# First layer's attention of a two-layer cross-attention kernel: scores in four 32-row strips, and another order of work round them

## What is computed

```python
def _L0_xattn_ref(q, latent_kv, Wq, Wkv_expand, Wout):   # q = layernorm(x), latent_kv = ctx_512 (first 100 rows matter: causal)
    NH, HD = 16, 16
    qp = q @ Wq.T
    kv = latent_kv @ Wkv_expand.T
    k, v = jnp.split(kv, 2, axis=-1)
    qh, kh, vh = [t.reshape(b, -1, NH, HD).transpose(0, 2, 1, 3) for t in (qp, k, v)]
    scores = jnp.einsum('bhqd,bhkd->bhqk', qh, kh) * inv_sqrt_d
    scores = jnp.where(causal, scores, jnp.finfo(scores.dtype).min)
    attn = jax.nn.softmax(scores, axis=-1)
    out = jnp.einsum('bhqk,bhkd->bhqd', attn, vh)
    return out.transpose(0, 2, 1, 3).reshape(b, sq, H) @ Wout.T
x = x + tanh(g_xattn[0]) * _L0_xattn_ref(layernorm(x), ctx_512, ...)
# then: mixture of 8 experts; second attention over 1444 keys; quantised feed-forward net. None of these is changed.
```

## Time and profile before

| | |
|---|---|
| median of three runs | 3318.08 us |
| profiled execution, its own time | 3316.05 us |
| its span | 3314.2 us |
| mean granted clock of TensorE | 0.932 |
| busy: PE, DVE, POOL, ACT | 87%, 74%, 53%, 45% |
| first layer's attention | first scores at 41.86 us, last addition to x ends at 443.0 us |

### The profile page before, as it was taken

One profiled execution on the slowest core, in us unless ns is written; L12 is line 12 of the kernel. 1 busy time (PEld: TensorE's weight loads), 2 busy tenths in 40 slices (PEclk: granted clock), 3 DMA queues, 4 the chain that ended last, 5 costly groups with the idle time before them and its releaser, 6 DMA issues. The chain is left out here.

```text
span 3314.2 us, 61706 instructions
## 1 busy us (share of the span) xinstructions
PE 2867.6 (87%) x18352; PEld 1925.3 (58%) x18352; DVE 2460.8 (74%) x4098; ACT 1485.7 (45%) x3074; POOL 1757.3 (53%) x1268
## 2 busy tenths in 40 slices
PE   5999979999798998998998999899899899896335
PEld 4777769999654555565565555556556456553123
DVE  5778754444388787887878878878788887876887
ACT  2333322222145545545545544554554554553556
POOL 0000022222267767767766666776775776764566
PEclk9889879999899999999999999999999999998566
DMA  4000010000300000000100000010010100011100
GB/s 112 0 0 0 0 48 10 10 5 10 80 11 16 21 12 21 19 16 17 24 17 16 21 19 17 16 26 7 21 26 11 22 19 16 11 48 31 47 13 24
DMA packets 130244, 71.05 MB, mean 21 GB/s; under 512 B 83582, under 2 KB 124510, under 8 KB 129880
## 3 DMA queue, kind: packets, MB, share of 16 engines
q1 hardware_dynamic: 129944, 67.45, 8.2%
HBM read 56.95 MB, written 10.04 MB: 20 GB/s over the span
## 5 line engine op out<-in xcount | busy, mean ns | idle before, releaser
L1195 POOL TENSOR_TENSOR c_psum<-c_p 120x800 f32<-120x800 f32 (+1 forms) x384 | 768.0, 2003 | 454.9 <-ACT c_p L1483 232.2
L1483 ACT ACTIVATE c_p<-c_s_ps 120x400 f32<-120x400 f32 (+1 forms) x1536 | 657.3, 507 | 475.6 <-PE c_s_ps L1644 458.0
L1279 DVE TENSOR_REDUCE c_mpart<-c_m_ps 128x1 f32<-128x484 f32 x1080 | 655.3, 650 | 159.6 <-PE c_m_ps L1551 158.1
L1656 PE MATMUL c_o_ps<-c_p,c_val 120*64 120x400 f32 (+1 forms) x3072 | 621.5, 528 | 0.0
L1306 DVE TENSOR_TENSOR c_acc<-c_acc,c_psum 120x800 f32<-120x800 f32 x256 | 398.2, 1555 | 53.0 <-POOL c_psum L1195 50.5
L1551 PE MATMUL c_m_ps<-c_kmax,c_q 64*128 64x484 f32 x1080 | 313.6, 463 | 114.9 <-DVE c_mpart L1279 93.8
L1186 POOL TENSOR_TENSOR l_rr<-c_psum,l_rr 96x400 f32<-96x400 f32 x256 | 260.6, 1039 | 193.5 <-DVE l_rr L1328 193.3
L1551 PEld LDWEIGHTS c_m_ps<-c_kmax,c_q 64*128 64x128 f32 x1080 | 139.2, 189 | 344.2 <-DVE c_mpart L1279 247.4
L1656 PEld LDWEIGHTS c_o_ps<-c_p,c_val 120*64 120x64 f32 (+1 forms) x3072 | 190.5, 138 | 251.5 <-issue 163.7
L1587 PE MATMUL c_s_ps<-c_xt,l_a 128*96 128x400 f32 x1536 | 310.3, 352 | 10.7 <-DVE l_rr L1328 8.2
L1640 PE MATMUL c_s_ps<-c_q,c_k 64*120 64x400 f32 (+1 forms) x1536 | 302.0, 366 | 2.3 <-ACT c_p L1483 2.3
(11 more groups left out here) (256 smaller groups left out, 4990.7 us busy)
## 6 DMA issues: line engine op xcount, KB each, us to landing
c_rdb<-l_denominators SPq DMA_DIRECT2D x128, 100.0 KB, 2.7
c_kv<-in_ctx SPq DMA_DIRECT2D x32, 360.0 KB
c_mrow<-c_mneg SPq DMA_DIRECT2D x288, 0.5 KB, 2.0
x_rows<-in_x SPq DMA_DIRECT2D x4, 800.0 KB
x_spill<-x_rows SPq DMA_DIRECT2D x8, 400.0 KB
l_xa<-x_spill SPq DMA_DIRECT2D x8, 400.0 KB
c_xr<-x_spill SPq DMA_DIRECT2D x32, 100.0 KB
x_spill<-c_xr SPq DMA_DIRECT2D x32, 100.0 KB
```

Source lines behind the costliest of these rows:

```text
L1195: g.tensor_tensor(psum[0:k, u % 2, :], p[0:k, 2 * u % 4, :], p[0:k, (2 * u + 1) % 4, :], ALU.add).then_inc(psum_ready, 1)
L1279: v.tensor_reduce(mpart[:, t, bank:bank + 1], m_ps[:, bank, 0:4 * KP], AX.X, ALU.max, negate=True).then_inc(mpart_ready, 1)
L1483: a.activation(p[0:k, w % 4, i * HALFQ:(i + 1) * HALFQ], s_ps[0:k, (2 * w + i) % 4, 0:HALFQ], ACT.Exp).then_inc(exp_ready, 1)
L1656: mm = pe.matmul(o_ps[i * DL:(i + 1) * DL, 0:HALFQ], val[0:k, j % 2, r, :], p[0:k, w % 4, i * HALFQ:(i + 1) * HALFQ], start=(r == 0), stop ...
```

## The change

The scores of one batch are made by eight matmuls of 32 rows and 200 columns in place of four of 128 rows and 400 columns. Quarter q now is what lies in partitions 32q to 32q+32 of both halves k of queries and keys, that is heads 2q, 2q+1 and 8+2q, 8+2q+1 (`heads(q)`); a pair of heads is kept apart by `parity`. The blocked keys of a whole group are written as the key products are evacuated (`kbd` holds 4 batches), half k = 0 by ACT, half k = 1 by DVE; `block_keys`, `kt` and `headsel` go. ACT also evacuates the values.

The order changes too. The dense products are renumbered (latents first, queries last). The masks are placed one by one as banks come free, and the eight score matmuls of batch b+1 stand together after the fourth mask, which waits for the last difference of batch b. DVE takes the differences of batch b in batch b, and `add_x(b - 2)` stands ahead of them.

Diff, cut to what matters:

```diff
-        kt = sb("a_kt", [128, KT, T])
-        kbd = [sb(f"a_kbd{i}", [128, KT, 8, S]) for i in range(2)]
+        kbd = sb("a_kbd", [128, KT, 2, T])
...
+        LATENTS, ROWS0, ROWS1, KEYS0, VALUES0, VALUES1, KEYS1, QUERIES0, QUERIES1 = range(9)
         ND = 9
+        VEC_OUT = (LATENTS, ROWS0, ROWS1, KEYS1, QUERIES0, QUERIES1)
+        ACT_OUT = (KEYS0, VALUES0, VALUES1)
+
+        def heads(q):
+            return [8 * k + 2 * q + e for k in range(KT) for e in range(2)]
...
-                    elif n < 5:
-                        v.tensor_copy(qt[:, n - 3, :], src).then_inc(dense_out, 1)
-                    elif n < 7:
-                        v.tensor_copy(kt[:, n - 5, :], src).then_inc(dense_out, 1)
+                        v.tensor_tensor(lo, src, hi.bitcast(F32), ALU.subtract).then_inc(vec_out, 1)
+                    elif n == KEYS1:
+                        for e in range(2):
+                            ins = v.tensor_scalar(kbd[:, 1, e, :], src, parity[:, e:e + 1], None, ALU.mult)
+                        ins.then_inc(vec_out, 1)
                     else:
-                        for j in range(2):
-                            ins = v.tensor_copy(va[:, 2 * (n - 7) + j, :, 0:HD],
-                                                s_ps[0:S, n % 4, j * D:(j + 1) * D].rearrange("p (h d) -> p h d", h=H))
-                        ins.then_inc(dense_out, 1)
-
-                def block_keys(it, b):
-
-                    if b >= 2:
-
-                        v.wait_ge(s_ready, PRIMED + (it * G + b - 1) * NQ)
-                    for k in range(KT):
-                        ins = v.tensor_tensor(kbd[b % 2][:, k], headsel[:],
-                                              kt[:, k, b * S:(b + 1) * S].unsqueeze(1).broadcast_to((128, 8, S)),
-                                              ALU.mult)
-                    ins.then_inc(kbd_ready, 1)
...
-                    block_keys(it, 1)
-                    for q in range(NQ):
-                        differences(0, q)
                     for b in range(G):
+                        if b >= 2:
+                            add_x(b - 2)
+                        if b == 1 and more:
+                            row_stats(it + 1)
+                        if b == 2 and more:
+                            normalise_rows(it + 1)
                         for q in range(NQ):
-                            if b + 1 < G:
-                                differences(b + 1, q)
-                            if b == G - 1 and more:
-                                for k in BESIDE_OUT[q]:
-                                    evacuate(it + 1, k)
-                            if q == 1 and b + 2 < G:
-                                block_keys(it, b + 2)
-                            if q == 2 and b > 0:
-                                add_x(b - 1)
-                            if q == 0 and b == 1 and more:
-                                row_stats(it + 1)
-                            if q == 0 and b == 2 and more:
-                                normalise_rows(it + 1)
-                        if b == G - 1 and more:
-                            v.wait_ge(dense_out, PRIMED + (it + 1) * ND + 7)
-                            block_keys(it + 1, 0)
-                        elif b == G - 1:
-                            split_moe()
-                        normalise(b)
+                            differences(b, q)
+                            if q == 1 and b > 0:
+                                normalise(b - 1)
+                            if b == G - 1 and more and q > 0:
+                                evacuate(it + 1, q - 1)
                     if more:
-                        for k in range(7, ND):
-                            evacuate(it + 1, k)
+                        add_x(G - 2)
+                        evacuate(it + 1, KEYS1)
+                        normalise(G - 1)
+                        evacuate(it + 1, QUERIES0)
+                    else:
+                        add_x(G - 2)
+                        split_moe()
+                        normalise(G - 1)
                     add_x(G - 1)
+                    if more:
+                        evacuate(it + 1, QUERIES1)
...
+                def evacuate(it, n):
+                    a.wait_ge(dense_mm, PRIMED + it * ND + n + 1)
+                    a.sem_inc(m.carrier, 1)
+                    if n == KEYS0:
+                        for e in range(2):
+                            ins = a.activation(kbd[:, 0, e, :], s_ps[:, n % 4, 0:T], ACT.Copy, scale=parity[:, e:e + 1])
+                    else:
+                        for j in range(2):
+                            ins = a.activation(va[:, 2 * (n - VALUES0) + j, :, 0:HD],
+                                               s_ps[0:S, n % 4, j * D:(j + 1) * D].rearrange("p (h d) -> p h d", h=H), ACT.Copy)
+                    ins.then_inc(act_out, 1)
...
-                            if q == 1 and b > 0:
+                                copy_pt(b, q - 1)
+                            if q == 2 and b > 0:
                                 copy_ct(b - 1)
-                        copy_pt(NQ - 1)
+                        if b == G - 1 and more:
+                            evacuate(it + 1, KEYS0)
+                        copy_pt(b, NQ - 1)
+                    if more:
+                        evacuate(it + 1, VALUES0)
+                        evacuate(it + 1, VALUES1)
...
+                def place_mask(q):
+                    pe.matmul(s_ps[0:S, q, 0:4 * S], identb[0:S, 0:S], mask[:].rearrange("p h k -> p (h k)"),
+                              start=True, stop=False, skip_group_check=True).then_inc(mask_done, 1)
+
+                def scores(it, b):
+                    pe.wait_ge(mask_done, PRIMED + (it * G + b + 1) * NQ)
+                    pe.sem_inc(m.carrier, 1)
+                    for k in range(KT):
+                        for q in range(NQ):
+                            rows = slice(32 * q, 32 * (q + 1))
+                            mm = pe.matmul(s_ps[0:S, q, 2 * k * S:2 * (k + 1) * S], qt[rows, k, b * S:(b + 1) * S],
+                                           kbd[rows, k, :, b * S:(b + 1) * S], start=False, stop=True, skip_group_check=True)
+                            if k == KT - 1:
+                                mm.then_inc(s_ready, 1)
+
+                def first_scores(it):
+                    act_done(it, VALUES1)
+                    place_mask(1)
+                    vec_done(it, KEYS1)
+                    place_mask(2)
+                    vec_done(it, QUERIES0)
+                    place_mask(3)
+                    vec_done(it, QUERIES1)
+                    place_mask(0)
+                    scores(it, 0)
...
-                    def scores(b, q):
-                        n = it * G * NQ + b * NQ + q
-                        pe.wait_ge(kbd_ready, PRIMED + it * G + b + 1)
-
-                        pe.wait_ge(diff_ready, PRIMED + n - NQ + 1 if b > 0 else it * G * NQ)
-                        o = s_ps[0:S, q, 0:4 * S]
-                        pe.matmul(o, identb[0:S, 0:S], mask[:].rearrange("p h k -> p (h k)"), start=True, stop=False)
-                        mm = pe.matmul(o, qt[:, q // 2, b * S:(b + 1) * S],
-                                       kbd[b % 2][:, q // 2, 4 * (q % 2):4 * (q % 2) + 4, :].rearrange("p h k -> p (h k)"),
-                                       start=False, stop=True)
-                        mm.then_inc(s_ready, 1)
...
-                    pe.wait_ge(dense_out, PRIMED + (it + 1) * ND)
-                    for q in range(NQ):
-                        scores(0, q)
...
                         for q in range(NQ):
-                            n = nb * NQ + q
                             if b + 1 < G:
-                                scores(b + 1, q)
-                            pe.wait_ge(prob_ready, PRIMED + n + 1)
-                            if b * NQ + q >= 2:
-                                pe.wait_ge(pt_copied, PRIMED + n - 1)
-                            for h in range(4):
-                                mm = pe.transpose(p_ps[0:S, q % 2, h * S:(h + 1) * S], prob[:, q, h, :], m.ident[0:S, 0:S])
-                            mm.then_inc(pt_ready, 1)
-                            if q == 0 and b > 0:
+                                pe.wait_ge(diff_ready, PRIMED + nb * NQ + q + 1)
+                                place_mask(q)
+                                if q == NQ - 1:
+                                    scores(it, b + 1)
+                            elif more:
+                                dense(it + 1, q)
+                            turn_probs(b, q)
+                            if q == 2 and b > 0:
                                 turn_out(b - 1)
-                            if q == 2 and b > 0:
+                            if q > 0:
+                                probs_value(b, q - 1)
+                            if q == 3 and b > 0:
                                 project_out(b - 1)
```

(107 more changed lines are left out.)

56 lines of the change are left out of this document (29 added, 27 removed).

## The result

The changed kernel takes 3468.3 us (median of 4 runs, 3465.55 to 3473.9) against 3315.74 us before (median of 4; a fourth run has joined the three named at the start). The ratio is 1.0457, 95% interval 1.0432 to 1.0482: 4.6% slower. The prediction was 3470 us, in a range of 3300 to 3545.

A forecast was written before the change was run, and what follows sets the result against it. PE bounds the kernel at 50.3 us per group; a lost clock makes that 69.9. Eight groups at 19.6 more, less 2 at the start, add 155 to 3316.05: 3470 us, range 3300 to 3545.

The forecast's parts named there:

- The chain of a group at full clock: First layer's attention, PE and DVE taking turns: four batches of 6.8, 11.8, 10.3 and 20.7 us, 49.6 us per group against 50.3.
- The scores, 1.5 us per batch: PE's 16 score records, partly overlapping across strips: 8 + 1 steps of 0.17 us, 1.5 us in place of 2.7.
- the faster rival: Strips overlap fully and the clock holds: a group takes 47.0 us, the kernel 3288 us; chance 0.14.
- The share at half clock, f = 0.7: Share of a group at 1.2 GHz in first layer's attention; a group takes 49.6 + 29 f, so 69.9 us.
- The group at half clock, 78.6 us: A group at 1.2 GHz throughout: PE's 36 us become 72, some 6 of waits remain; 29 us more.
- The drain at a change of the tiling mode: TensorE drains at two mode changes per batch, estimated 0.17 us each: 1.4 us per group, 11 in all, not summed.
- Lockstep at full clock: Rival: strips count as full work for the clock, which stays as it is; 3308 us, up to 3340; chance 0.10.
- the strips would not overlap: Rival: scores stay 2.7 us per batch, a group 54.4 us at full clock; 3347 us, over 3550 at half; chance 0.05.
- The clock row: Sign: PE's clock at 5 to 7 tenths in slices 1 to 6; the prediction is wrong if it stays at 9.
- the wait for the projection: Sign: DVE waits about 5 us before the addition to x at the third and fourth batch, released by the projection.
- the wait for the scores at every batch's first reduce: Sign on DVE: at each batch's first reduce it waits for L402; no size given.
- Later phases: Sign: the phases after the first layer's attention should keep their lengths.

## Why the prediction was right

- *The chain of a group at full clock, 49.6 us*: 48.9 measured, with fillers in it, so the order alone is at most that. Batch by batch it is 7.0, 11.2, 9.9 and 20.8 us where the chain had 6.8, 11.8, 10.3 and 20.7, and `add_x` waits 4.46 and 4.38 us where it had about 5. With the shorter scores (next point) the sum would be 47.1; most of the other 1.8 us lies in the first and the last batch, and whether fillers or links of the chain take them was not taken apart.
- *The scores, 1.5 us per batch*: too long. The 16 records take 0.87 us from their start to that of the next work at full clock (below) and 1.59 at half (339.25 to 340.84), where the step had 3.0. That is full overlap, which only the faster rival had: four steps of 0.17 and 0.2 more. The Trainium skill (TensorE: Matmul & The Clock Gate, Measured speedup vs the span model) has 3.07 times for four strips, measured with 512 columns. Here, with 200 columns, it is 2.76 / 0.87 = 3.2, and the trace agrees. So this term was 0.6 us too large at full clock, 1.4 at half, four times a group.

Timeline of PE in the run with add_x later and 88 fillers:

```profile
153.75 0.33 PE L397 MATMUL a_s_ps<-a_mask,a_identb 100*100 100x400 bf16 x1
154.23 0.94 PE L406 MATMUL a_s_ps<-a_kbd,a_qt 32*100 32x200 f32 x16
155.10 0.55 PE L443 MATMUL a_p_ps<-ident,a_prob 100*100 100x100 f32 x4
```

- *The share at half clock, f = 0.7*: too small, 0.92. The clock does come back with the queries, as predicted, but only when the second of the two products is nearly done, and goes some 7 us later.
- *The group at half clock, 78.6 us*: too long. From 69.4 = 0.92 x h + 0.08 x 48.9 follows h = 71.2, 7.4 less; 5.6 of it are the scores, and the rest is open. The waits that remain at half clock are 6.1 us per group, where the step had some 6. The two errors cancel: with f = 0.92 alone the sum would have been 49.6 + 0.92 x 29 = 76.3 per group and 3316 + 8 x 26.0 - 2 = 3522 us; the shorter group at half clock brings it back to 69.4. The mechanism is as predicted, and that the number fell within 2 us of the median is partly luck.
- *The drain at a change of the tiling mode* (11 us at most, left out of the sum): the run with 128-row scores and 128 fillers has no such change at the scores and can be set beside this one. Ahead of the scores there is no difference: 0.48 us from the mask's start to theirs in both (172.10 to 172.58, 153.75 to 154.23). Behind them, 0.87 is 0.19 over 4 steps of 0.17, and 2.76 is 0.04 over 16. So some 0.15 us per batch at most, 5 us in all, where 11 had been the bound.
- *The rivals.* Lockstep at full clock would have given 3308; what it needs, the held clock, the changed kernel has in no group. Faster strips did happen, but the clock did not hold with them. That the strips would not overlap is refuted (7.3 us per group).
- *The signs.* The clock row and the wait for the projection came. PE's row did not: 7 to 9 tenths where 5 to 8 were expected, for at half clock the same work fills it. Nor did the wait for the scores at every batch's first reduce: 14 times in 28 batches, for at the third and fourth batch `add_x` has waited already.
- *Later phases* keep their length, as predicted: the next phase's first DVE instruction starts at 443.58 us before and 591.95 after, and from there to the end it is 2870.6 and 2873.6 us. Over the traces of all these kernels the part behind the last addition takes 2864 to 2881 us, so totals can differ by some 10 us for reasons that are not in this phase; the group times above do not have that.

How far each effect goes: with add_x where the change has it, holding the clock gives 20.5 us per group (69.4 to 48.9); moving add_x and dropping 11 fillers then gives another 4.5 (to 44.4). The move by itself gave 1.9 where the fillers were too many (53.7 to 51.8), and 3.5 without the clock (69.4 to 65.9). What is not settled is how the fall divides between the fewer rows of the scores and the waits; the run with 128-row scores restored a part of the clock (0.73) and not all, so a stronger drive in the scores has a share and is not the whole. That run also makes the scores three times as long, and rows and length were not tested apart there.

## What to carry to other kernels

Packing a matmul into row strips makes it shorter, and it can take away work that helped to keep the clock up: look at what PE drives in the stretch that is left, not only at how full its row is. If waits remain, full-height fillers placed in them can be worth far more than they cost, but in this phase too few were worth almost nothing (35 per group; 64 that were not placed by the waits), and too many lay on the path (128). An addition that waits for the last product of a batch should not stand ahead of the first work of the next.

## What was not expected of the hardware

- The four strips run wholly side by side even though each instruction has two records on its own strip: 16 records in 0.87 us at full clock. In the trace they start in four bunches of four, at 154.23, 154.46, 154.62 and 154.79. The later strips' first records did not wait for the earlier strip's second, as I had assumed from the earlier trace rows.
- The clock depended on the rows driven more sharply than thought: at 99% busy with 32-row fillers it stayed at 0.54, with 128-row fillers at the same places it was 0.99; 57 fillers per group gave 1.00, 35 gave 0.60.
